# A decoder's last stage: keys and values made in the stage before it, and the other weight products placed between its first tiles

## The reference, cut to what matters

```python
def _L1_attn_ref(x, time_decay, time_first, ..., W_k, W_v, W_r, W_o):
    # a decaying average over time, token after token
    k = jnp.einsum('bth,oh->bto', xk, W_k)
    v = jnp.einsum('bth,oh->bto', xv, W_v)
    r = jax.nn.sigmoid(jnp.einsum('bth,oh->bto', xr, W_r))
    wkv = _wkv_full(k, v, time_decay, time_first)
    return jnp.einsum('bth,oh->bto', r * wkv, W_o)

def _L1_xattn_ref(hidden_states, key_value_states, Wq, bq, Wk, bk, Wv, bv, Wo, bo, stride):
    Q = (hidden_states @ Wq.T + bq)      # 16 heads of 32
    K = (key_value_states @ Wk.T + bk)   # 128 context tokens, 8 for each head
    V = (key_value_states @ Wv.T + bv)
    ...
    attn = jax.nn.softmax(scores, axis=-1)
    out = jnp.einsum('bhqk,bhkd->bhqd', attn, Vg)
    return out @ Wo.T + bo

def _L1_ffn_ref(x, Wq, routers, leaf_keys, leaf_values, Wout_w, Wout_b):
    # a soft decision tree of depth 8: 255 gates, 256 leaves
    ...
```

## Time and profile before

| what | value |
|---|---|
| device time, median of 3 runs | 2828.28 us (2824.74 to 2835.46) |
| span of the profiled execution | 2826.6 us; no device time of its own is listed beside it |
| PE busy | 2548.6 us (90%) |
| DVE busy | 2224.5 us (79%) |
| ACT busy | 1417.6 us (50%) |
| mean granted TensorE clock | 0.970 |

### The profile page before, as it was taken

One profiled execution on the slowest core, in us unless ns is written; L12 is line 12 of the kernel. 1 busy time (PEld: TensorE's weight loads), 2 busy tenths in 40 slices (PEclk: granted clock), 3 DMA queues, 4 the chain that ended last, 5 costly groups with the idle time before them and its releaser, 6 DMA issues. The chain is left out here.

```text
span 2826.6 us, 83010 instructions
## 1 busy us (share of the span) xinstructions
PE 2548.6 (90%) x35304; PEld 1801.5 (64%) x35304; DVE 2224.5 (79%) x4027; ACT 1417.6 (50%) x2569; POOL 512.1 (18%) x661
## 2 busy tenths in 40 slices
PE   6788989899898979999999987997799999989998
PEld 5566666666666756777677654443377777766765
DVE  3898988889998628888887784987778888871886
ACT  7667666777566213323333223545366666651554
POOL 2233322233223210000000000004511111120222
PEclk9999999999999989999999999999899999998999
DMA  2001111111111221121220114548932122123332
GB/s 89 21 16 34 56 34 41 34 34 56 34 41 63 100 97 41 53 75 53 75 68 31 60 60 145 186 158 290 315 118 75 61 61 89 61 75 105 119 121 74
DMA packets 165805, 234.24 MB, mean 83 GB/s; under 512 B 17858, under 2 KB 94018, under 8 KB 162884
## 3 DMA queue, kind: packets, MB, share of 16 engines
q1 hardware_dynamic: 165444, 229.01, 24.6%
HBM read 136.18 MB, written 92.80 MB: 81 GB/s over the span
## 5 line engine op out<-in xcount | busy, mean ns | idle before, releaser
L612 PE MATMUL delta_banks<-both_columns,both_mats 128*128 128x256 f32 x1536 | 383.5, 394 | 5.7 <-ACT both_line L865 4.8
L612 PEld LDWEIGHTS delta_banks<-both_columns,both_mats 128*128 128x128 f32 x1536 | 278.9, 191 | 48.9 <-ACT both_line L865 8.0
L883 ACT ACTIVATE both_product<-both_line,delta_conv_w 128x256 f32<-128x256 f32 x576 | 248.6, 496 | 7.1 <-DVE both_conv L1105 6.2
L1512 PE MATMUL ctxatt_banks<-both_product,ctxatt_oT 128*128 128x512 f32 x512 | 228.4, 599 | 4.9 <-DVE both_conv L1627 4.9
L1473 PE MATMUL ctxatt_banks<-both_line,both_mats 128*128 128x256 f32 x960 | 221.5, 384 | 1.3 <-SPq L1424 1.3
L1473 PEld LDWEIGHTS ctxatt_banks<-both_line,both_mats 128*128 128x128 f32 x960 | 180.5, 193 | 24.8 <-SPq L1424 1.6
L1162 DVE TENSOR_TENSOR delta_squares<-delta_t_sys 128x30 f32<-128x30 f32 (+14 forms) x480 | 175.0, 365 | 12.5 <-issue 0.2
L1165 DVE TENSOR_TENSOR delta_t_sys<-delta_t_sys,delta_squares 128x30 f32<-128x30 f32 (+14 forms) x480 | 165.4, 345 | 16.5
L865 ACT ACTIVATE both_line<-delta_banks,delta_proj_b 128x256 f32<-128x256 f32 x192 | 87.8, 457 | 170.3 <-PE delta_banks L612 170.1
L1512 PEld LDWEIGHTS ctxatt_banks<-both_product,ctxatt_oT 128*128 128x128 f32 x512 | 95.3, 191 | 115.5 <-issue 109.0
L1559 ACT ACTIVATE ctxatt_probsT<-ctxatt_banks 128x512 f32<-128x512 f32 x128 | 69.5, 594 | 189.3 <-PE ctxatt_banks L1494 189.2
(11 more groups left out here) (366 smaller groups left out, 5816.6 us busy)
## 6 DMA issues: line engine op xcount, KB each, us to landing
h<-ffn_hid SPq DMA_DIRECT2D x66, 256.0 KB, 2.1
xT<-both_newT SPq DMA_DIRECT2D x24, 512.0 KB, 3.6
x<-both_new SPq DMA_DIRECT2D x24, 512.0 KB, 4.0
x<-decay_last SPq DMA_DIRECT2D x24, 512.0 KB, 7.3
ffn_hid<-h SPq DMA_DIRECT2D x6, 1536.0 KB, 8.3
both_columns<-xT SPq DMA_DIRECT2D x16, 512.0 KB, 4.9
delta_x<-x SPq DMA_DIRECT2D x16, 512.0 KB, 4.0
both_line<-xT SPq DMA_DIRECT2D x16, 512.0 KB, 4.6
```

What stands on the lines that cost most here:

```text
L612: mm = pe.matmul(b_proj[:, p % 2, 0:B * P], wT[NAMES[i]][:, k, g * P:(g + 1) * P], xT_sb[:, n.parity, k], start=k == 0, stop=k == KB - 1)
L883: made = act.activation(slot(n, i)[:, j - 1, g].rearrange("p (b t) -> p b t", b=B), line[:, i, g, :, j:j + P], ACT.Copy, scale=conv_w[:, i ...
L1512: mm = pe.matmul(b_o[:], oT[:, b, k, :], wo[:, k, :], start=k == 0, stop=k == PAIRS - 1)
```

## The change

The eight products of keys and values move into the decaying average's last steps. On PE `later_product(0)` stands at the end of step 17, products 1, 2 and 3 after `turn_new(13, 1)` in step 18, product 4 at the start of step 19, 5 and 6 after `turn_new(14, 1)`, and 7 after `turn_new(15, 0)`, ahead of `turn_new(15, 1)`. They use banks 3, 5, 1 and 4. DVE's `keep_later` stands around `add(15, 0)` and after the moments of tile 15. The keys and values go into the half of the tile `mixed` that the last tile doesn't use, and so `mixed` moves to `AttentionWeights`, which outlives the stage.

In the last stage only the first five products (query weights and query bias) stand ahead of the tiles. The other eight stand inside steps 1 to 4 of PE, and ACT's copies of them in its steps 0 to 3. The wait for all copies becomes three waits of the first tile: `scores` for 5 copies, `attend` for 7, `gates` for all 13. The banks of the products are chosen by hand. SP issues the first tile's columns ahead of the tree's weights.

```diff
+                def later_product(i):
+                    if i == 0:
+                        pe.wait_ge(key_kept, QUADS * WSTEPS)
+                    elif i == 1:
+                        pe.wait_ge(r_kept, QUADS * WSTEPS)
+                    elif i < 4:
+                        q = i - 2
+                        pe.wait_ge(averaged[q], AVG_OPS * (WSTEPS - 1) + FRESH)
+                        pe.wait_ge(taken_made, QUADS * (WSTEPS - 1) + q + 1)
+                    else:
+                        pe.wait_ge(kv_kept, i - 3)
+                    t, e = i // KB, i % KB
+                    for k in range(KB):
+                        mm = pe.matmul(banks[:, KV_BANKS[i % 4], 0:B * CTX], later.mats[("wkT", "wvT")[t]][:, k, e * P:(e + 1) * P],
+                                       later.cT[:, k].rearrange("p b n -> p (b n)"), start=k == 0, stop=k == KB - 1)
+                    mm.then_inc(kv_made, 1)
...
                     if t2:
                         project(t2, 0, 0)
+                    if last:
+                        later_product(4)
                     if t5:
                         turn_new(t5, 1)
+                    if ending:
+                        later_product(1)
+                        later_product(2)
+                        later_product(3)
+                    if last:
+                        later_product(5)
+                        later_product(6)
...
                     if t3:
                         output(t3, 1)
+                    if n.index == WSTEPS + 1:
+                        later_product(0)
+                    if last:
+                        later_product(7)
...
+                    if ending:
+                        keep_later(0)
                     if t3:
                         add(t3, 0)
+                    if ending:
+                        keep_later(1)
+                        keep_later(2)
+                        keep_later(3)
+                    if last:
+                        keep_later(4)
+                        keep_later(5)
+                        keep_later(6)
+                        keep_later(7)
...
+        PRODUCT_BANKS = (0, 1, 2, 3, 4, 5, 6, 4, 7, 5, 4, 7, 5)
...
                     if n:
                         load_columns(n)
+                    if n.index == 0:
+                        load_weights()
...
+                    if i == 0:
+                        pe.wait_ge(ready, 3)
+                    if i == ROUTER:
+                        pe.wait_ge(tree_here, 16 * TREE_LOADS)
+                    earlier = [j for j in range(i) if PRODUCT_BANKS[j] == PRODUCT_BANKS[i]]
+                    if earlier:
+                        pe.wait_ge(kept, earlier[-1] + 1)
...
                     if t1:
                         scores(t1)
+                    if n.index == 1:
+                        product(VALUE)
+                        product(VALUE + 1)
+                        product(ROUTER)
+                    if n.index == 2:
+                        product(ROUTER + 1)
                     if t2:
                         turn_probabilities(t2)
+                    if n.index == 2:
+                        product(ROUTER + 2)
+                    if n.index == 3:
+                        product(ROUTER + 3)
+                        product(LEAF)
+                    if n.index == 4:
+                        product(LEAF + 1)
...
-                multiply_weights()
+                for i in range(BIAS + 1):
+                    product(i)
                 unrolled(pe, STEPS, 6, step)
```

More of the change, by code:

```diff
@@ L2697, in add, with keep_later @@
                     dve.tensor_tensor(norm.y[:, r], banks[:, OUT_BANK + r], x_sb[:, n.parity, r], ALU.add).then_inc(norm.done, 1)
+                def keep_later(i):
+                    t, e = i // KB, i % KB
+                    if i == 0:
+                        dve.wait_ge(later_here, 16 * later.LOADS)
+                    dve.wait_ge(kv_made, i + 1)
+                    for b in range(B):
+                        op = dve.scalar_tensor_tensor(
+                            later.kv[t][:, e, b, :], banks[:, KV_BANKS[i % 4], b * CTX:(b + 1) * CTX], later.cols["bk" if t == 0 else "bv"][:, e:e + 1],
+                            later.mask[:, e, t, :], ALU.add, ALU.mult)
+                    op.then_inc(kv_kept, 1)
                 def step(n):
                     t1, t2, t3, t4 = n.back(1), n.back(2), n.back(3), n.back(4)
+                    ending, last = n.index == WSTEPS + 2, n.index == WSTEPS + 3
                     if t4:
@@ L2789, in __init__ @@
         self.bo_row = tile("bo_row", [1, D])
+        self.mixed = tile("mixed", [P, 2, 3, KB, B, WT])
+        spare = self.mixed[:, 0].rearrange("p i k b t -> p (i k b t)")
+        self.kv = [spare[:, i * KB * B * CTX:(i + 1) * KB * B * CTX].rearrange("p (k b n) -> p k b n", k=KB, b=B) for i in range(2)]
         self.LOADS = 4 + 1 + 3 + 1 + 1 + 1
@@ L2935, in _ @@
             def _(pe):
[L2936 to L2968, removed]
@@ new lines, in product @@
+                def product(i):
+                    bank = banks[PRODUCT_BANKS[i]]
+                    if i == 0:
+                        pe.wait_ge(ready, 3)
[4 more added lines that the diff above has]
+                        pe.wait_ge(kept, earlier[-1] + 1)
+                    if i < BIAS:
+                        for e in range(KB):
+                            mm = pe.matmul(bank[:, 0:B * CTX], mats["wq"][:, e, i * P:(i + 1) * P], kv[0][:, e].rearrange("p b n -> p (b n)"),
+                                           start=e == 0, stop=e == KB - 1)
+                    elif i == BIAS:
+                        for e in range(KB):
+                            mm = pe.matmul(bank[0:1, 0:B * CTX], cols["bq"][:, e:e + 1], kv[0][:, e].rearrange("p b n -> p (b n)"),
+                                           start=e == 0, stop=e == KB - 1)
+                    elif i < ROUTER:
+                        for e in range(KB):
+                            pe.matmul(bank, kv[1][:, e, i - VALUE, :], mats["woT"][:, e, :], start=e == 0, stop=False)
+                        mm = pe.matmul(bank, share_row[:], bo_row[:], start=False, stop=True)
+                    elif i < LEAF:
+                        c = i - ROUTER
+                        for e in range(KB):
+                            mm = pe.matmul(bank[:, 0:LEAVES], mats["fq"][:, e, c * P:(c + 1) * P], routersT[:, e, :], start=e == 0, stop=e == KB - 1)
+                    else:
+                        l = i - LEAF
+                        for e in range(KB):
+                            pe.matmul(bank, leafT[:, e, l * P:(l + 1) * P], mats["outT"][:, e, :], start=e == 0, stop=False)
+                        mm = pe.matmul(bank, ones_row[:], wb_row[:], start=False, stop=True)
+                    mm.then_inc(made, 1)
@@ L3119, in step @@
                         exps(n)
+                    if n.index == 0:
+                        keep_product(VALUE)
+                        keep_product(VALUE + 1)
+                        keep_product(ROUTER)
+                    if n.index == 1:
+                        keep_product(ROUTER + 2)
                     if t2:
                         finish_attention(t2, 0)
-                keep_products()
+                    if n.index == 2:
+                        keep_product(ROUTER + 3)
+                        keep_product(LEAF)
+                act.wait_ge(ready, 3)
+                for i in range(BIAS + 1):
+                    keep_product(i)
                 unrolled(act, STEPS, 6, step)
@@ L3231, in step @@
                         walk_tree(t3, 1)
-                keep_keys_and_values()
+                dve.wait_ge(ready, 3)
                 unrolled(dve, STEPS, 5, step)
```

60 lines of the change are left out of this document (33 added, 27 removed).

## The result

| | before | changed |
|---|---|---|
| median, first comparison | 2831.87 us (4 runs) | 2814.36 us (4 runs) |
| ratio, first comparison | | 0.9931, 95% interval 0.9912 to 0.9950 |
| median, repeated on another occasion | 2829.49 us (11 runs) | 2812.23 us (6 runs) |
| ratio, repeated | | 0.9943, 95% interval 0.9928 to 0.9958 |
| profiled execution, span | 2826.6 us | 2812.1 us |

The changed kernel is faster: by the first ratio 0.0069 x 2832 = 19.5 us, by the second 16 us. 18.2 us was predicted. A ratio on record is not exactly the quotient of the two medians: that is 0.9938 and 0.9939, inside both intervals, or 17.5 and 17.3 us. The first interval ends at 0.9950, where the prediction put the bound of what can be told from no change, and the second a little beyond it. The profiled execution of the changed kernel took 2813.84 us, 1.7 us more than its span.

The account below looks back on a forecast made before the run. PE was taken to bound the kernel. Drain +1.8, boundary +0.5, moved products -13.8 and fill -6.7 gave -18.2 us, from a median of 2828.3 to 2810 us, range 2805 to 2822.

Parts of the forecast that it names:

- the bound of what can be told from no change: Whole kernel: a measurement can tell about 0.5%, 14 us, from no change, so faster means below 2814.1 us.
- The bound: Steady last stage: PE always busy at full clock, so a microsecond taken ahead of it moves the end by one.
- The drain: Decaying average's last steps: eight products of 13.8 us go mostly into PE's gaps, ending the drain 1.8 us later.
- The walk in program order: Drain: PE's new order stepped through at full-clock strides; last transposes end at 2546.0 where they ended at 2544.2.
- The boundary: Between drain and last stage: the first product now waits for the last memset, costing 0.5 us.
- The front and the fill: Last stage up to the fifth scores: 13.8 us of products leave, 6.7 us won between first tiles.
- The slow start: Last stage's first products: 2.8 us lost because PE starts at the lower clock, assumed to remain.
- the 7.6 us: First tiles, up to `scores(3)`: 7.6 of 19.5 us idle or at 1.2 GHz, idle parts being waits for DVE and ACT.
- The loads: First router product: weights land by 2566, product comes at 2574.0, so eight microseconds to spare.
- the fourth rival: Router product: weights come late and PE stops, a microsecond per microsecond; slower by 0.5% is 2842 us; chance 0.04.
- The second rival: First tiles: the clock falls to 1.2 GHz, costing 2.7 to 5 us, total 2813 to 2815 us; chance 0.20.
- the section of the Trainium skill: First tiles: PE working through banks in short groups with small pauses can swing between clock levels; weighed against the change.

Follow-up runs that it names:

- e1: Kernel before with only the key and value products moved into the drain, the other 13 all ahead of the first tile; ratio 0.9965 to before.
- e5: Changed kernel with no key or value product ahead of the drain's last output, products 0 to 3 right behind it; ratio 0.9949 to before.
- e2: Changed kernel with keys and values made ahead of the first tile again, eight products still between the tiles; ratio 0.9982 to before.
- e3: Kernel before with only PE's one wait for all 13 copies split into waits of the first tile's steps; ratio 0.9988 to before.
- e11: Changed kernel with only PE's wait for the memsets moved from the first product to the first scores; one run, 2808.06 us.
- e7: Changed kernel with the eighth product behind the last tile's second transposes and the memset wait moved to the first scores; ratio 0.9932 to before.
- e6: Changed kernel with SP issuing the tree's weights two steps later, behind the third tile's columns; ratio 0.9941 to before.
- e9: The changed kernel itself timed once more, nothing edited; ratio 0.9943 to before.
- e10: The same kernel as e7, changed kernel with eighth product last and memset wait moved, run once more; ratio 0.9934 to before.
- e4: The kernel before run once more for a second trace, nothing edited; one run, 2826.2 us.
- e8: Kernel before with only the memory placement of the change (mixed inputs, keys and values), instruction order as before; one run, 2836.71 us.

## Why the prediction was right

**The bound.** PE sets the end of the last stage: what was taken from it ahead of the steady part came off the end. The distance from the fifth scores to the end stayed, but for 1.7 us at the very end.

**The drain, +1.8 predicted, +1.9 measured.** The walk in program order gave the result; e1 has the same drain, e5 shows that the place in the gaps is what pays. One thing in it was less firm than I wrote: "in the drain an idle 3.73 us was enough for the clock to leave the full level" held in three traces of the old order and not in e2, e3 and e5, with the same idle time. In those the old drain is 26.6 us where it could be seen whole (e2, e3), and against it the change costs 3.7, not 1.9. The three traces with the order of before all have the slow output, though, so the +1.9 is what this pair of kernels shows.

**The boundary, +0.5 predicted, +0.5 measured** (3.35 to 3.88 us), and e11 takes it away again.

**The front and the fill, -20.5 predicted, -21.3 measured.** The slow start, which I kept at 2.8, cost 1.8, and its place moved. Before, the clock fell while the last transposes of the drain ran and stayed at half over the whole boundary; after, it was full over the boundary and fell only when the first product had begun. Windows of before, then of the changed kernel (busy PE, clock, DMA share, GB/s):

```profile
2546.00:2547.00 1.00, 0.00 (x0) 0.50 1.01 271
```

```profile
2555.00:2556.00 1.00, 0.04 (x1) 1.00 1.08 327
2557.00:2558.00 1.00, 1.00 (x4) 0.50 0.96 235
```

So "PE started at the lower clock" is true of before and not of after, and that 1.8 us were lost again is no sign that the step was right: over all 13 traces the loss went from 0.1 (e7) to 3.2 us (e1). The fill itself gave what was said, 6.4 for 6.7: three scores and what goes with them took 12.1 us without the products, 11.9 predicted, and the waits are 0.55 ahead of the scores, for 0.69, and 0.19 at the gates, for 0.2, of which the second costs 0.5, as e2 shows. What I did not weigh rightly is what the 7.6 us consisted of. Of the earlier trace rows and the rows between them, 2.8 us were idle PE (0.69, 1.22 and twice 0.47), and some 4 us matmuls at 1.2 GHz, and the second part depends on when the clock falls: e3, without moving any work, had 2.5 less of it and e1 1.1 less. So the reason that the prediction gave, work that covers PE's waits for DVE and ACT, accounts for the smaller part of the gain. The larger is matmuls at the full clock; that it stays full goes with the products between the tiles in all seven traces in which no load came late, but these runs don't show by what.

**The loads, eight microseconds to spare.** The weights landed at 2570.83 and the router product came at 2578.94, so the margin was 8.1 us, as predicted. e6 shows what stands behind it: the fourth rival's mechanism is real, its condition wasn't met. That the first tile's columns now go ahead of the weights was not tested by itself. The first scores didn't wait for the columns in either kernel: what they wait for last is ACT's copy, before and after.

**The clock over the first tiles.** The second rival, with 2 in 10, did not come: in the changed kernel, e9, e10, e11, e7, e2 and e5 the granted clock was 1.00 over the first tiles. With all products ahead of the tiles it was 0.73 to 0.74 in the three traces of the order before, 0.82 in e1 and 0.90 in e3. In e6 it fell once, around the 4.54 us of waiting for the weights. So the section of the Trainium skill that I had weighed against the change ("TensorE: Matmul & The Clock Gate", "A second HAM failure mode: psum-queue depth-cycling") fits the old fill better than the new one: there, short groups with pauses between them went with one fall of the clock in each of five traces, and the same groups with products between them with none in seven. The steady stage, which I held against the section, tests it less than I wrote, since PE has no pauses there (20.00 of 20 us busy).

**The rest, 1.7 us at the end of the span.** The last eight matmuls took 5.40 us before and 3.70 after, at the clock of the moment. It was not predicted, and no run shows that it is an effect of the change: e5, e6 and e10, all with the new order in the last stage, have the slow end too (199.5 to 199.6 from the fifth scores), and e3, with the old one, has not (197.9). But the three traces of the order before all have it and the two of the changed kernel have not, so the runs don't exclude it either. Without it the changed kernel won 18.8 us in the trace, for the 18.2 predicted.

Clock luck in the trace and scatter of some 15 us in the stages ahead explain why the total, at 16 to 19.5 us with intervals of 8 to 11 us width, can't check terms of 2 us; only distances inside the trace could.

## What to carry to other kernels

Where a stage starts with work that needs none of the stage's input, look for idle time on its engine on both sides of the barrier: in the drain ahead (products that need only early loads) and between the first tiles' steps. Walk the engine's program in order to see what each insertion delays, and put the last piece behind the instruction on which the final store hangs. Note the margin of every load that a moved product now waits for, since it stands ahead of the pipeline where before it stood only ahead of other products. And compare distances inside the trace, between instructions that both kernels have, when the total scatters by more than the terms.

## What the runs showed of the hardware that was not expected

The same idle time on PE may or may not be followed by the lower clock: 3.73 or 3.74 us ahead of one group of eight 128x512 matmuls was followed by 6.23 to 6.27 us for them in three traces and by 3.67 in three others. The slow three are those with the order of before (before, e4, e8), the fast ones e2, e3 and e5. A boundary with 2.0 us idle gave a full-clock start in one trace and a slow one in the next of the same kernel. And a fall of the clock need not show in the gap itself: in the changed kernel it was 1.00 over the idle boundary and half only after the first product had begun. And the clock fell at 2600.9 before, with PE idle for only 0.69 us but with one-row matmuls on both sides; without the 0.69 us (e3) it fell near 2606, behind the 1.22 us of waiting for DVE. What exactly decides isn't settled by these runs.
